# A graph attention layer with layer norm: column means prepared by VectorE, and both ends put in another order

## The reference, cut to what matters

```python
# x: (16, 512, 384), adj: (16, 512, 512) bool, 12 heads of 32 columns
h = einsum('bnd,ade->bane', x, W);  th = tanh(h)
attn = einsum(th, w_src) + swapaxes(einsum(th, w_dst))
attn = where(attn >= 0, attn, 0.2 * attn)
attn = where(~adj, -999.0, attn);  attn = softmax(attn, axis=-1)
feat = elu(einsum('banm,bame->bane', attn, h) + b)
gate = sigmoid(x @ H_w.T + H_b)
y = gate * feat + (1 - gate) * x
out = layernorm(x + y)
```

## Time and profile before

| | |
|---|---|
| median of 3 runs | 671.02 us |
| the profiled execution | 670.99 us |
| its span in the trace | 668.9 us |
| granted TensorE clock, mean | 0.994 |

### The profile page before, as it was taken

How to read it: one execution, slowest core, us unless ns; L and a number is a source line. 1 busy time by engine, 2 the same in 40 slices (tenths; PEclk the granted TensorE clock), 3 DMA queues, 4 the chain that set the end, 5 groups by cost and what they waited for, 6 DMA issues and landing times.

```text
span 668.9 us, 12479 instructions
## 1 busy us (share of the span) xinstructions
PE 646.2 (97%) x3279; PEld 366.9 (55%) x3279; DVE 646.5 (97%) x1171; ACT 447.7 (67%) x936; POOL 565.1 (84%) x444
## 2 busy tenths in 40 slices
PE   8999999999999999999999999999999999998982
PEld 5554656555565555555555555565656556564530
DVE  7999999999999999999999999999999999999796
ACT  5524558587675867767586775858677585966754
POOL 2536898989989998998989999899989989896482
PEclk9999999999999999999999999999999999999997
DMA  6336558568485766847586585857758485765502
GB/s 205 117 100 196 174 128 235 159 168 243 146 239 139 224 169 164 228 157 233 145 214 180 147 240 144 234 136 202 216 145 227 136 244 140 205 179 146 202 31 95
DMA packets 54715, 117.62 MB, mean 176 GB/s; under 512 B 7074, under 2 KB 32420, under 8 KB 54692
## 3 DMA queue, kind: packets, MB, share of 16 engines
q1 hardware_dynamic: 42180, 81.56, 37.7%
q0 software_dynamic: 4320, 23.59, 18.8%
q10 hardware_dynamic: 8192, 12.19, 5.4%
HBM read 104.35 MB, written 12.98 MB: 175 GB/s over the span
## 4 chain that ended last, share of the span: by engine, by line
PE 80%; ACT 9%; DVE 5%; issue 3%; DMA 1%; POOL 1%; ACTq 0%; SPq 0%; POOLq 0%; DVEq 0%
PE out_T L1022 43%; PE hg L930 30%; PE tr L1030 6%; ACT xT_hi L460 3%; ACT scratch L550 3%; DVE ew L789 2%; ACT att_T L522 2%; DVE sd L751 1%; DMA xT_in<-in_xT 1%; DVE th_w L736 1%; PE hg L960 1%; PE hg L964 0%; ACT scratch L557 0%; POOL th_w L296 0%; DVE hb_sum L725 0%
## 5 line engine op out<-in xcount | busy, mean ns | idle before, releaser
L789 DVE SCALAR_TENSOR_TENSOR ew<-v_all,u,adj 128x512 f32<-128x512 f32 x768 | 524.8, 727 | 1.9 <-DMA v_all<-v_rows 0.9
L1022 PE MATMUL out_T<-ew,vals 128*64 128x512 f32 x1536 | 356.4, 599 | 0.0
L1022 PEld LDWEIGHTS out_T<-ew,vals 128*64 128x64 f32 x1536 | 105.2, 136 | 186.9 <-issue 146.7
L296 POOL TENSOR_TENSOR th_w<-th,score_w 128x768 f32<-128x768 f32 x58 | 127.9, 2206 | 23.4 <-DVE th_w L736 10.2
L522 ACT ACTIVATE att_T<-out_T,out_bias 128x512 f32<-128x512 f32 x96 | 66.1, 689 | 105.1 <-PE out_T L1022 104.7
L930 PE MATMUL hg<-w_hi,xT_hi 128*128 128x384 f32 x384 | 99.5, 367 | 2.7 <-ACT xT_hi L460 1.5
L930 PEld LDWEIGHTS hg<-w_hi,xT_hi 128*128 128x128 f32 x384 | 61.7, 191 | 52.8 <-issue 50.7
L930 PE MATMUL hg<-w_lo,xT_hi 128*128 128x384 f32 x384 | 88.6, 338 | 0.0
L930 PE MATMUL hg<-w_hi,xT_lo 128*128 128x384 f32 x384 | 87.7, 335 | 0.0
L930 PEld LDWEIGHTS hg<-w_lo,xT_hi 128*128 128x128 f32 x384 | 69.5, 188 | 0.0
L930 PEld LDWEIGHTS hg<-w_hi,xT_lo 128*128 128x128 f32 x384 | 68.9, 188 | 0.0
(11 more groups left out here) (116 smaller groups left out, 681.4 us busy)
## 6 DMA issues: line engine op xcount, KB each, us to landing
v_all<-v_rows SPq DMA_DIRECT2D x95, 512.0 KB, 4.7
xT_in<-in_xT SPq DMA_DIRECT2D x16, 768.0 KB, 9.3
h_sb<-in_bias POOLq DMA_DIRECT2D x15, 768.0 KB, 6.6
x_in<-in_x SPq DMA_DIRECT2D x15, 768.0 KB, 4.6
gate_tanh<-in_H_b POOLq DMA_DIRECT2D x15, 768.0 KB, 9.5
out<-y ACTq DMA_DIRECT2D x15, 768.0 KB, 3.8
adj_in<-in_adjT SPq DMA_DIRECT2D x16, 256.0 KB, 9.5
v_rows<-v_turn SPq DMA_DIRECT2D x64, 6.0 KB
```

Of the source, the lines that this page charges most:

```text
L296: g.tensor_tensor(th_w[:, c % 2], th[:, c].unsqueeze(1).broadcast_to([P, 2, D]), score_w[:], ALU.mult).then_inc(S["thw_done"], 1)
L789: ve.scalar_tensor_tensor(out=ew[:, (2 * C * j + i) % SLOTS, :], in0=v_all[:, j % VSLOTS, k], scalar=u[:, q, c, h:h + 1], in1=ADJ[c][:], o ...
L1022: te.matmul(OUT[VW * k:VW * k + VW, :], vals[:, q, c, h, :], ew[:, t % SLOTS, :], start=(c == 0), stop=(c == C - 1)).then_inc(S["ew_free"], 1)
```

## The change

Four things change.

1. *Means.* After GpSimd has written `hb_tot`, VectorE transposes it in 32x32 blocks (128x384, into the first half of `hb_sum`, now named `hb_turn`) and sums each block's 32 columns, which gives `mean_part` (128x12). This `mean_parts` stands at index 0 of head pair 5 in steps 0 to 14. TensorE's `means` becomes one product of `mean_part` with a constant `mean_sel` (128x128, built by GpSimd at the start with one memset and seven selects), twelve columns wide. `out_biases` needs two copies (32x6) in place of four (32x3), except for graph 0, which keeps the old form.
2. *Step 0.* The two `head_products` on VectorE go to GpSimd; VectorE's sums for these chunks are then of the folded half, 384 columns. GpSimd's subtraction for `gate_bias` moves behind the bias DMA of step 0.
3. *Last step.* TensorE does `gates(0)` ahead of the transpose of the last pair of graph 14. ScalarE takes `gates_last(1)` ahead of `copy_out(1)`, and `gate_quarter` ahead of `copy_out(2)`. VectorE's `inverses` for pair 0 of graph 15 stands two `ew` later.
4. *Tail.* VectorE's gate, rest and statistics for MIDDLE are put ahead of or beside the last pair, so that only FINAL (64 columns) is left behind it; the statistics are in three parts instead of two. Each of the two last stores becomes two, one a chunk.

```diff
+            def mean_parts(b, q):
+                dve.wait_ge(S["hb_sum_done"], 2 * b)
+                ve.transpose(hb_turn, hb_tot[:, q]).then_inc(S["hb_turned"], 1)
+                dve.wait_ge(S["hb_turned"], b)
+                if not isinstance(b, int) or b > 1:
+                    dve.wait_ge(S["hm_done"], b)
+                ve.tensor_reduce(mean_part[:], hb_turn.rearrange("p (h k) -> p h k", k=VB), AX.X, ALU.add).then_inc(S["part_done"], 1)
...
+                    if j == 5 and not last:
+                        between[0] = [lambda: mean_parts(b + 1, 1 - q)]
...
             def means(b, q):
-                pe.wait_ge(S["hb_sum_done"], 2 * b)
+                pe.wait_ge(S["sel_done"], 2 * (P // VB))
+                pe.wait_ge(S["part_done"], b)
                 pe.wait_ge(S["gate_done"], C * b)
-                for i in range(H // 4):
-                    last = te.matmul(mean_ps[:, i:i + 1], hb_tot[:, q, i * P:(i + 1) * P], mean_w[:, 0:1],
-                                     start=True, stop=True)
-                last.then_inc(S["hm_done"], 1)
+                te.matmul(mean_ps, mean_sel[:], mean_part[:], start=True, stop=True).then_inc(S["hm_done"], 1)
...
             def add_rows(b, q):
                 pool.wait_ge(S["add_bias_done"], 16 * b)
+                if not isinstance(b, int) or b > 1:
+                    pool.wait_ge(S["part_done"], b - 1)
...
+                m = mean_ps.rearrange("p (j k) -> p k j", k=2)
+                for k in range(2):
+                    rows = slice(VW * k, VW * k + E)
+                    a.activation(out_bias[rows, q], m[rows, k], ACT.Copy).then_inc(S["out_bias_done"], 2)
...
                     if j == 1 and first:
-                        between[3] = [lambda: head_products(1, 0), lambda: head_sums(1, 0)]
-                        between[8] = [lambda: head_products(1, 1), lambda: head_sums(1, 1)]
+                        between[3] = []
+                        between[5] = [lambda: head_sums(1, 0)]
...
-                        at = (None, 6, 5, 7, 7, 6)[j]
+                        at = (None, 6, 7 if last else 5, 7, 7, 6)[j]
...
                 gates_last(b, 0)
                 x_forms(b - 1)
                 normalise(b - 2)
+                gates_last(b, 1)
                 copy_out(b, q, 1)
-                gates_last(b, 1)
                 gates_last(b, 2)
                 x_last_form()
                 gates_last(b, 3)
+                gate_quarter(b)
                 copy_out(b, q, 2)
-                gate_quarter(b)
...
                 dve.wait_ge(S["gate1_done"], B)
                 elu_late(0, MIDDLE)
+                gated(MIDDLE, 1)
                 dve.wait_ge(S["y_early_done"], 2)
+                with_rest(MIDDLE, 1)
                 statistics(0, EARLY)
                 inverses()
                 quotients()
-                gated(MIDDLE, 1)
+                dve.wait_ge(S["y_late_done"], 2)
+                statistics(1, MIDDLE)
                 elu_late(1, FINAL)
                 gated(FINAL, 2)
-                y = y_last[:, :, LATE]
-                dve.wait_ge(S["y_late_done"], 2)
-                ve.tensor_tensor(y, y, rest_last[:, :, LATE], ALU.add).then_inc(S["y_late_done"], 1)
-                dve.wait_ge(S["y_late_done"], 3)
-                statistics(1, LATE)
+                with_rest(FINAL, 3)
+                dve.wait_ge(S["y_late_done"], 4)
+                statistics(2, FINAL)
...
             def step_last(b, q):
+                gates(b, q, 0, True)
                 transpose_out(b - 1, HP - 1)
-                gates(b, q, 0, True)
                 attend(b, q, 0)
```

More of the change, by code:

```diff
@@ L95, in gat_layernorm @@
         bias_row = sb("bias_row", [P, E])
+        mean_sel = sb("mean_sel", [P, P])
+        mean_part = sb("mean_part", [P, H])
         zeros = sb("zeros", [P, P], BF16)
@@ L114, in gat_layernorm @@
         squares = sb("squares", [P, C])
-        stats = sb("stats", [P, C, 2, 6])
+        stats = sb("stats", [P, C, 3, 6])
         mv = sb("mv", [P, C, 2])
@@ L120, in gat_layernorm @@
         shift = sb("shift", [P, C])
+        hb_turn = hb_sum[:, 0]
         x_last = xT_in[:].rearrange("p k n -> p (k n)").rearrange("p (c d) -> p c d", d=D)
@@ L140, in gat_layernorm @@
         d_max = HG[0][:, 2 * P:2 * P + H]
-        mean_ps = HG[1][:, D:D + H // 4]
+        mean_ps = HG[1][:, D:D + H]
         mean_first_ps = TR[:, 0:H // 4]
@@ L145, in gat_layernorm @@
         names = """st_last ld_w ld_wg ld_cols ld_hb ld_xT ld_x ld_adj st_y st_v ld_v0 ld_v1 ld_v2 ld_b bias_first rows_first spread_first spread_copied
-            pool_setup dve_setup adj_done gate_bias_split gate_bias_done
-            w_hi_done w_lo_done xhi_done xlo_done h_done th_done thw_done thh_done sd_done hcopy_done g_done gate_done add_gate_bias tanh_done add_bias_done hb_sum_done hm_done
+            pool_setup sel_done dve_setup adj_done gate_bias_split gate_bias_done
+            w_hi_done w_lo_done xhi_done xlo_done h_done th_done thw_done thh_done sd_done hcopy_done g_done gate_done add_gate_bias tanh_done add_bias_done hb_sum_done hb_turned part_done hm_done
             scores mxT_done mxb_done exps_done v_turned vals_done
@@ L157, in gat_layernorm @@
         FINAL = slice(5 * VW, D)
-        LATE = slice(3 * VW, D)
         def feature_bank(b, c):
@@ L252, in after @@
             def after():
[L253 to L256, removed]
+                for c in range(2, C):
+                    sp.wait_ge(S["last_y_done"], c - 1)
+                    sp.dma_start(out_v[B - 1][:, c], y_last[:, c]).then_inc(S["st_last"], 16)
+                sp.wait_ge(S["st_y"], 16 * B + 32)
+                sp.wait_ge(S["st_last"], 32)
             program(sp, step, before, after)
@@ L265, in before @@
                 g.sem_inc(S["mixed"], 3)
-                g.sem_inc(S["thh_done"], 2)
                 g.memset(gate_bias_in, 0.0).then_inc(S["pool_setup"], 1)
                 g.memset(ident[:], 0.0).then_inc(S["pool_setup"], 1)
+                g.memset(mean_sel[:], 0.0).then_inc(S["sel_done"], 1)
                 g.memset(mean_w[:], TINY / N).then_inc(S["pool_setup"], 1)
@@ L277, in before @@
                 pool.wait_ge(S["pool_setup"], 10)
+                pool.wait_ge(S["sel_done"], 1)
                 g.affine_select(out=ident[:], in_=ident[:], compare_op=ALU.not_equal, fill=1.0, base=0,
                                 pattern=[[-1, P]], channel_multiplier=1).then_inc(S["pool_setup"], 1)
+                for t in range(1 - P // VB, P // VB):
+                    if t > 1 - P // VB:
+                        pool.wait_ge(S["sel_done"], t + P // VB)
+                    g.affine_select(out=mean_sel[:], in_=mean_sel[:], compare_op=ALU.not_equal, fill=TINY / N, base=VB * t,
+                                    pattern=[[-1, P]], channel_multiplier=1).then_inc(S["sel_done"], 1)
                 g.memset(vals[:, 1], 0.0).then_inc(S["pool_setup"], 1)
@@ L286, in before @@
                     split_low(1, 1, c)
-                pool.wait_ge(S["gate_bias_split"], 2)
-                g.tensor_tensor(gate_bias[:], gate_bias_in, gate_bias_off, ALU.subtract).then_inc(S["gate_bias_done"], 1)
             def weigh(b, c):
                 pool.wait_ge(S["th_done"], C * b + c + 1)
[L292 to L295, removed]
+                pool.wait_ge(S["sd_done"], C * b + c - 1)
                 g.tensor_tensor(th_w[:, c % 2], th[:, c].unsqueeze(1).broadcast_to([P, 2, D]), score_w[:],
@@ L318, in add_rows @@
                 pool.wait_ge(S["add_bias_done"], 16 * b)
+                if not isinstance(b, int) or b > 1:
+                    pool.wait_ge(S["part_done"], b - 1)
                 g.tensor_tensor(hb_sum[:], h_sb[:, 0:2], h_sb[:, 2:4], ALU.add).then_inc(S["hb_sum_done"], 1)
                 pool.wait_ge(S["hb_sum_done"], 2 * b - 1)
-                if not isinstance(b, int) or b > 1:
-                    pool.wait_ge(S["hm_done"], b - 1)
+                if not isinstance(b, int) or b > 2:
+                    pool.wait_ge(S["hb_turned"], b - 2)
+                elif b == 2:
+                    pool.wait_ge(S["hm_done"], 1)
                 g.tensor_tensor(hb_tot[:, q], hb_sum[:, 0], hb_sum[:, 1], ALU.add).then_inc(S["hb_sum_done"], 1)
@@ L390, in step @@
                 if not last:
-                    for c in range(2 if first else 0, C):
+                    for c in range(C):
                         weigh(b + 1, c)
@@ L394, in step @@
                     add_bias(b + 1)
+                if first:
+                    pool.wait_ge(S["gate_bias_split"], 2)
+                    g.tensor_tensor(gate_bias[:], gate_bias_in, gate_bias_off, ALU.subtract).then_inc(S["gate_bias_done"], 1)
                 if not first:
@@ L507, in out_biases @@
                     act.wait_ge(S["outT_copied"], HP * (b - 1))
[L508 to L512, removed]
+                if isinstance(b, int) and b == 0:
+                    m = out_bias[:, q].rearrange("p (i s) -> p i s", s=2)
```

(34 more changed lines are left out.)

## The result

The changed kernel takes 674.57 us (median of 5 runs, 674.52 to 676.39) against 671.02 us before. The ratio is 1.0058, with a 95% interval of 1.0043 to 1.0072. It is slower by 3.55 us; 674.6 had been forecast. The profiled execution took 674.54 us, 672.7 us of it in the span, 3.8 us more than before.

What follows compares the result with a forecast made beforehand. VectorE's own work took 38.79 us of a 39.28 us step, TensorE leading by at most 0.49. Terms +16.1 - 6.3 - 2.6 - 3.2 - 0.4 = +3.6 on 671.0 gave 674.6 us; 8-in-10 range 668.8 to 679.8.

Steps and rivals of the forecast that it cites:

- pair on VectorE: Steps 0 to 14: new transpose and reduction of 384 columns cost VectorE 1.07 us each time, 16.1 us (11.9 to 20.7).
- given back in steps 1 to 14: VectorE's idle time, at most 0.49 us a step, recovered at 0.45 in 14 steps: 6.3 us (4.8 to 6.9).
- step 0: First step: VectorE has 3.5 us less, then waits 0.9 for TensorE; 2.6 us gained (1.5 to 3.5).
- last step: Last step: VectorE waits 0.4 us for TensorE's transpose instead of 3.63; 3.2 us gained (1.2 to 3.6).
- tail and stores: Behind the last weights: net 0.1 us on VectorE, 0.3 from split stores; 0.4 us gained (-0.5 to 1.5).
- Rival C: New means: dearer transposes, 1.38 us for transpose plus reduction, 20.7 us in all; 679.2 us. Chance 0.12.
- TensorE's gain: Means on TensorE: at most 0.1 us a step, since the next transpose needs ScalarE's copy anyway.
- The sign I had named: Steady middle: VectorE's busy time at 99.5% or more, its waits for transposes gone.
- there in time: Steady steps: once VectorE is the slower engine, TensorE catches up and its transposes no longer keep VectorE waiting.
- A: Whole kernel: new transpose and reduction are hidden, the ends' 6.2 us count; 664.8 us. Chance 0.15 (664 to 669.7).
- D: New means: VectorE waits 0.5 us for GpSimd's `hb_tot` in each of 14 steps; 681.6 us. Chance 0.05.
- B: Whole kernel: near a tie, by a cheap transpose (670.4 us) or the ends' upper bounds (672.2). Chance 0.15.

Runs made afterwards that it cites:

- ends_only: Changed kernel with the old means (three products on TensorE, no transpose or reduction on VectorE, four small ScalarE copies): 664.58 us, ratio 0.9902.
- means_only: Kernel before with the new means alone, both ends in the old order: 680.59 us, ratio 1.0141.
- three_products: Changed kernel with TensorE's one means product of twelve columns issued three times: 674.94 us, ratio 1.0056.
- late_pair: Changed kernel with the reciprocal of head pair 1 one weight later in steps 0 to 14 (index 6 instead of 5 of pair 2): 671.59 us, ratio 1.001.
- step0_only: Kernel before with step 0 alone changed (both score products and the gate bias moved on GpSimd): 668.32 us, ratio 0.996.
- tail_only: Kernel before with the tail alone changed (VectorE's order behind the last weights, three statistics, split stores): 670.16 us, ratio 0.9988.

## Why the prediction was right

The forecast of 674.6 us met the time by 0.03 us. The mechanism is the one forecast: the pair costs more than VectorE's idle time holds, TensorE gains nothing, and the ends pay part. That it came so close is luck in the terms: what was given back was put 1.1 us too high, and the small errors of the others and of what lies outside the span made up 1.0 of it.

| Term | predicted | measured |
|---|---|---|
| pair on VectorE, 15 times | +16.1 (1.07 each) | +15.9 (1.06 each) |
| given back in steps 1 to 14 | -6.3 | -5.2, what is left of the span |
| step 0 | -2.6 | -2.8 |
| last step | -3.2 | -3.2 |
| tail and stores | -0.4 | -0.6 |

With 0.15 us by which the first `ew` starts earlier, the measured terms give the 3.8 us of the span. In the time it is 3.55, since less lies outside the span, 1.84 us instead of 2.09. (The table is rounded; 5.2 comes from the unrounded terms.)

*The pair.* The slope of the reduction carried over to the transpose: 0.57 us forecast, 0.556 measured. Rival C is out. The Trainium skill's rate of one element per cycle (Vector Engine (DVE) Microarchitecture Reference, "The reshape front-end and per-opcode configuration") gave 0.56; the trace agrees. `ends_only` and `means_only` give its net cost, 10.0 and 9.5 us, against 16.1 - 6.3 = 9.8.

*TensorE's gain.* None, as forecast; `three_products` and the 0.57 us wait for ScalarE's copy show it.

*What was given back.* Here the sum was near and the reason half wrong. I expected VectorE's idle time to go from 0.49 us a step to almost none. It went to 0.34 (4.27 us in 12.54 steps), 2.1 us in 14 steps. The sign I had named, VectorE busy 99.5% and its waits gone, did not come: it is 99.1%, with 12 waits. The transposes were to be "there in time"; one of them, at index 5 of pair 2, is not. `late_pair` shows that this is what was left, 3.0 us in all. Most of the rest came from an instruction that I hadn't looked at: the ELU, 1788 ns on average after the change (`ex`, above) and 2043 before, 0.25 us a step, 3.6 us in 14. Its group before the change, 100 to 600 us:

```profile
L811 DVE SCALAR_TENSOR_TENSOR ex<-ex,att 128x1536 f32<-128x1536 f32 x13 | 26.6, 2043 | 0.0
```

The two make 5.7 us. The 14 steps with their 14.8 us of pairs grew by 9.7, so 5.1 came back there, like the 5.2 left in the sum; the 0.5 or so between stays unexplained. Held against `ends_only` it is 15.9 - 10.0 = 5.9, since the ends, read from VectorE's rows, come to 6.8 us and bring only 6.2 of span. So 3.6 us of a term that came out near 5 have a reason that the prediction didn't have.

*Step 0.* 57.05 for the pair's place against 60.03 before, less 0.15 by which the first `ew` starts earlier. VectorE waits 0.47 us at the reciprocal for TensorE, where 0.9 was forecast, and 0.24 us for GpSimd, where none was. VectorE came to the reciprocal at 41.6, as forecast; the transpose it needs came at 41.47 and not at 41.85, since `attend(1)` starts at 36.20 instead of 36.61, for the reason that `step0_only` shows.

*Last step.* A wait of 0.39 us in place of 3.63; 0.4 had been forecast, from `copy_out(0)` as the link that is late next. That link shows in TensorE's 0.82 us.

*Tail.* From the end of the last `ew` to the end of the span 13.3 us against 13.9. On VectorE it is 0.1, the forecast; the stores give 0.5, not 0.3, close to the upper bound. The trace of `tail_only` has the same two parts; the order and the stores weren't tried one without the other.

```profile
662.80 0.19 DVE L824 RECIPROCAL rden<-tr 128x8 f32<-128x8 f32 x1
...
665.51 0.60 DVE L883 BATCH_NORM_STATS2 stats<-ex 128x6 f32<-128x64 f32 x4
```

The wait of 0.65 us ahead of this reciprocal is gone, filled by work moved ahead.

*Rivals.* A (hidden pair, 664.8) falls: what was to be its time is that of `ends_only`, where the pair is left out. D (a wait for `hb_tot`) falls: neither the transpose nor the reduction has a listed wait. B falls in both its ways: the transpose isn't cheaper, and the ends bring 6.5 us, not 8.6.

## What to carry to other kernels

Two engines were busy 97% here, and yet one of them led. Look in the steady middle which of the two still has waits, and take its idle time a step as the most that it can take on. Work moved onto it costs what goes beyond that; here 1.06 us were put where 0.49 was free, and what was taken off TensorE lay under another engine's copy. Time one part of a change at a time: six and a half good microseconds were hidden under ten bad ones.

## What was not expected of the hardware

The ELU (two SBUF inputs, 1536 columns) takes VectorE 1.75 to 2.37 us, by how much of a GpSimd instruction is still ahead of it. In the kernel before, steps 1 and 4 (`th_w<-th_w` is GpSimd's fold, `th_w<-th,score_w` its next product):

```profile
71.20 1.01 POOL L302 TENSOR_TENSOR th_w<-th_w 128x384 f32<-128x384 f32 x1
72.18 1.75 DVE L811 SCALAR_TENSOR_TENSOR ex<-ex,att 128x1536 f32<-128x1536 f32 x1
72.35 3.29 POOL L296 TENSOR_TENSOR th_w<-th,score_w 128x768 f32<-128x768 f32 x1
...
189.76 1.01 POOL L302 TENSOR_TENSOR th_w<-th_w 128x384 f32<-128x384 f32 x1
190.01 2.37 DVE L811 SCALAR_TENSOR_TENSOR ex<-ex,att 128x1536 f32<-128x1536 f32 x1
190.72 3.37 POOL L296 TENSOR_TENSOR th_w<-th,score_w 128x768 f32<-128x768 f32 x1
```

In step 4 the fold runs for another 0.76 us after the ELU has started, to 190.77, and the ELU ends 1.61 us after that. In step 3 it runs for another 0.30, and the ELU takes 1.91, again ending 1.61 us after the fold. In step 1 only 0.03 us are left of the fold, and the ELU takes 1.75. GpSimd's product takes 3.3 to 3.4 us in each case instead of 1.84; in step 4 it ends 1.71 us after the ELU. This fits the two engines standing for each other, the ELU until the fold is done and the product until the ELU is. The Trainium skill (GPSIMD Engine Reference, "Specifications") names this contention for VectorE's instructions with two SBUF inputs; the trace agrees.

In the changed kernel the ELU stands later against GpSimd's order, with 0.08 us of the fold left at 309.88, and takes 1.75. That step 1 of the kernel before has the short ELU too speaks for the position and against anything else in the change; it wasn't tried by itself. The six kernels with TensorE in the lead whose groups were read have 2032 to 2059 ns on average, the five with VectorE in the lead 1786 to 1794, but these five all have the pair as well.
